# Gate scaling of half of each expert tile moved from ScalarE to GpSimd, between the tile's result scatters

## The reference

```python
x = x + 0.5 * ffn(layernorm(x))
x = x + attention(layernorm(x))
x = x + 0.5 * ffn(layernorm(x))
```

```python
topv_aK, topi_aK = jax.lax.top_k(x_aD @ router_DE, 2)
gates_Ea = sigmoid(masked scores).T          # -inf where not chosen
routed_in_EaD = x_aD[None] * gates_Ea[:, :, None]
h_EaF = silu(einsum('ead,edf->eaf', routed_in_EaD, w_in_eDF)) \
        * einsum('ead,edf->eaf', routed_in_EaD, w_swiglu_eDF)
out_aD = shared_out_aD + sum_over_e(einsum('eaf,efd->ead', h_EaF, w_out_eFD))
```

## Time and profile before

| what | value |
| --- | --- |
| runs | 1060.45 us median (1058.06 to 1062.33) |
| profiled execution | span 1057.9 us (the page gives no time beside it) |
| mean granted clock of TensorE | 0.915 |
| busy: PE, DVE, ACT, POOL | 864.0, 637.0, 562.7, 654.4 us |
| chain that ended last, by engine | PE 59%, ACT 11%, DVE 10%, unknown 10%, issue 5%, POOL 3% |

### The profile page before, as it was taken

The page is one execution under the profiler, slowest core; times in us unless marked ns, Lnnn a source line. Parts: engine busy times, 40 slices in busy tenths (PEclk is TensorE's granted clock), DMA queues, the critical chain, the costliest instruction groups (busy, mean ns, idle before and its releaser), DMA issues.

```text
span 1057.9 us, 19428 instructions
## 1 busy us (share of the span) xinstructions
PE 864.0 (82%) x5857; PEld 744.1 (70%) x5857; DVE 637.0 (60%) x2022; ACT 562.7 (53%) x1678; POOL 654.4 (62%) x669
## 2 busy tenths in 40 slices
PE   4655665658898888837999999997698988898898
PEld 3544555557888888833777776776598888898787
DVE  6644655454555555425798988885555554564586
ACT  4321422205655565528988888872165655565432
POOL 4656366453676776666088887666447666676551
PEclk9877787788999999978999999997889999899989
DMA  9511011043333333225012211111433233232484
GB/s 230 170 39 46 26 46 43 33 79 90 86 84 89 88 86 84 80 74 160 1 57 77 75 59 39 37 41 36 89 80 94 83 87 92 81 84 74 128 255 125
DMA packets 112920, 88.01 MB, mean 83 GB/s; under 512 B 13426, under 2 KB 102132, under 8 KB 112820
## 3 DMA queue, kind: packets, MB, share of 16 engines
q1 hardware_dynamic: 94816, 51.08, 19.1%
q0 software_dynamic: 17280, 35.69, 10.3%
q10 hardware_dynamic: 724, 0.01, 0.0%
HBM read 43.68 MB, written 43.04 MB: 82 GB/s over the span
## 4 chain that ended last, share of the span: by engine, by line
PE 59%; ACT 11%; DVE 10%; another core or an unknown queue 10%; issue 5%; POOL 3%; DMA 2%; SPq 0%; ACTq 0%; DVEq 0%
PE bank L927 12%; PE bank L1391 5%; PE bank L911 5%; PE bank L1367 4%; PE bank L909 4%; PE bank L910 4%; PE bank L917 4%; PE bank L1377 3%; ACT XG L865 2%; POOL results L837 2%; ACT SG L884 2%; PE bank L720 2%; PE bank L650 2%; PE bank L206 1%
## 5 line engine op out<-in xcount | busy, mean ns | idle before, releaser
L837 POOL DMA_INDIRECT results<-YO,XS x284 | 306.0, 1077 | 167.6 <-ACT YO L876 95.4
L818 DVE TENSOR_TENSOR HT<-bank,SG 128x512 f32<-128x512 f32 x142 | 98.3, 692 | 181.9 <-PE bank L911 88.3
L408 POOL DMA_INDIRECT pairs<-PAY,POS x128 | 126.5, 988 | 97.8 <-DVE POS L241 60.6
L909 PE MATMUL bank<-XSH,WX 128*128 128x256 f32 x568 | 175.2, 309 | 3.8 <-issue 3.7
L1017 POOL DMA_INDIRECT pairs<-PAY,POS x128 | 136.2, 1064 | 63.1 <-issue 32.9
L910 PE MATMUL bank<-XSL,WX 128*128 128x256 f32 x568 | 162.9, 287 | 3.8 <-issue 3.7
L911 PE MATMUL bank<-XSH,WX 128*128 128x256 f32 x568 | 162.7, 287 | 0.7 <-issue 0.4
L927 PE MATMUL bank<-WOE,HT 128*128 x1136 | 156.8, 282 | 0.2
L927 PEld LDWEIGHTS bank<-WOE,HT 128*128 128x128 f32 x1136 | 140.1, 194 | 5.0 <-issue 1.0
L865 ACT ACTIVATE XG<-XS 128x128 f32<-128x128 f32 x284 | 113.7, 402 | 21.6 <-DMA XS<-pairs 21.5
L910 PEld LDWEIGHTS bank<-XSL,WX 128*128 128x128 f32 x568 | 111.0, 195 | 5.4 <-issue 5.3
(11 more groups left out here) (197 smaller groups left out, 1825.3 us busy)
## 6 DMA issues: line engine op xcount, KB each, us to landing
XS<-pairs SPq DMA_DIRECT2D x142, 130.0 KB
Y<-results SPq DMA_DIRECT2D x32, 256.0 KB
YF<-results SPq DMA_DIRECT2D x32, 256.0 KB, 4.2
results<-YO,XS POOLq DMA_INDIRECT x284
pairs<-PAY,POS POOLq DMA_INDIRECT x256
out<-X SPq DMA_DIRECT2D x16, 256.0 KB, 3.0
pairs<-pad_rows SPq DMA_DIRECT2D x16, 130.0 KB
pairs<-pad_rows SPq DMA_DIRECT2D x1, 1040.0 KB
```

Source lines behind the costliest of these rows:

```text
L408: pool.indirect_dma_start(pairs, bass.IndirectOffsetOnAxis(ap=POS[:, b % RB, j, c:c + 1], axis=0), PAY[:, b % RB, c, j, :], None).then_inc ...
L818: dve.tensor_tensor(HT[:, i % 2, :], bank[4 + i % 2][:, :], SG[:, i % 2, :], ALU.mult)\
L837: pool.indirect_dma_start(results, bass.IndirectOffsetOnAxis(ap=XS[:, u, j, AT_DEST:AT_DEST + 1].bitcast(U32), axis=0), YO[:, u, j, :], No ...
L909: pe.matmul(ps, WX[:, i % 2, 1, w], hi, start=True, stop=False)
```

## The change

In both expert stages the gate scaling of each tile's second half (j = 1) is taken from ScalarE and given to GpSimd, as a `tensor_scalar` multiplication. ScalarE keeps the first half. On GpSimd the multiplication of tile i + 5 stands between the two scatters of tile i; those of the first five tiles stand ahead of all scatters. XG grows from two to three buffers. TensorE's transposes wait for both engines, by a semaphore for each, and GpSimd waits for the rows (xs_loaded) and for the transposes that last read its XG buffer (xs_turned).

```diff
--- before.py
+++ after.py
@@ -145,7 +145,7 @@
             "table_done pads_known pads_written padded "
             "std1 stats1 normed xt_turned xt_copied xt_split scored topped gate_raw gated picked ranked "
             "rank_taken pay1 pay2 placed up0 up1 silu0 silu1 hid0 hid1 down shared_added xt_high weights_high "
-            "xs_scaled xs_turned xs_high xs_low e_weights e_up0 e_up1 e_silu e_hid e_down e_out "
+            "xs_scaled xs_scaled2 xs_turned xs_high xs_low e_weights e_up0 e_up1 e_silu e_hid e_down e_out "
             "summed a_added a_stats a_log a_rstd a_shift a_normed a_turned a_copied q_made k_made v_made "
             "q_ready k_ready v_ready weighed updated r_stats r_log r_rstd kept_split combined").split())
         x_loaded = sems("x_loaded", len(GROUPS))
@@ -761,7 +761,7 @@
                 mem = ctx if ffn else own
                 XS = sb(f"XS{ffn}", [P, XB, 2, ROW], mem=mem)
                 YO = sb(f"YO{ffn}", [P, XB, 2, D], mem=mem)
-                XG = sb(f"XG{ffn}", [P, 2, 2, D], mem=mem)
+                XG = sb(f"XG{ffn}", [P, 3, 2, D], mem=mem)
                 XSH = sb(f"XSH{ffn}", [P, 2, 2 * P], F32R, mem=mem)
                 XSL = sb(f"XSL{ffn}", [P, 2, 2 * P], F32R, mem=mem)
                 WX = sb(f"WX{ffn}", [P, 2, 2, 2 * F], F32R, mem=mem)
@@ -830,13 +830,29 @@
 
                 @block.gpsimd
                 def _(pool):
-                    for i in range(NT):
+                    def scale(i):
+                        pool.wait_ge(xs_loaded[slot(i)], 16 * (turns(i) + 1))
+                        if i >= 3:
+                            pool.wait_ge(k["xs_turned"], done + i - 2)
+                        pool.tensor_scalar(XG[:, i % 3, 1, :], XS[:, slot(i), 1, 0:D],
+                                           XS[:, slot(i), 1, AT_GATE:AT_GATE + 1], None, ALU.mult)\
+                            .then_inc(k["xs_scaled2"], 1)
+
+                    def scatter(i, j):
                         u = slot(i)
-                        pool.wait_ge(k["e_out"], done + i + 1)
-                        for j in range(2):
-                            pool.indirect_dma_start(
-                                results, bass.IndirectOffsetOnAxis(ap=XS[:, u, j, AT_DEST:AT_DEST + 1].bitcast(U32), axis=0),
-                                YO[:, u, j, :], None).then_inc(y_sent[u], 16)
+                        if j == 0:
+                            pool.wait_ge(k["e_out"], done + i + 1)
+                        pool.indirect_dma_start(
+                            results, bass.IndirectOffsetOnAxis(ap=XS[:, u, j, AT_DEST:AT_DEST + 1].bitcast(U32), axis=0),
+                            YO[:, u, j, :], None).then_inc(y_sent[u], 16)
+
+                    for i in range(-5, NT):
+                        if i >= 0:
+                            scatter(i, 0)
+                        if i + 5 < NT:
+                            scale(i + 5)
+                        if i >= 0:
+                            scatter(i, 1)
 
                 @block.sync
                 def _(sp):
@@ -859,11 +875,10 @@
 
                 @block.scalar
                 def _(act):
-                    def scale(i, j):
-                        if j == 0:
-                            act.wait_ge(xs_loaded[slot(i)], 16 * (turns(i) + 1))
-                        act.activation(XG[:, i % 2, j, :], XS[:, slot(i), j, 0:D], ACT.Copy,
-                                       scale=XS[:, slot(i), j, AT_GATE:AT_GATE + 1]).then_inc(k["xs_scaled"], 1)
+                    def scale(i):
+                        act.wait_ge(xs_loaded[slot(i)], 16 * (turns(i) + 1))
+                        act.activation(XG[:, i % 3, 0, :], XS[:, slot(i), 0, 0:D], ACT.Copy,
+                                       scale=XS[:, slot(i), 0, AT_GATE:AT_GATE + 1]).then_inc(k["xs_scaled"], 1)
 
                     def high(i):
                         act.wait_ge(k["xs_turned"], done + i + 1)
@@ -876,20 +891,17 @@
                         act.activation(YO[:, slot(i), :, :].rearrange("p j d -> p (j d)"), bank[6 + i % 2][:, 0:2 * D],
                                        ACT.Copy, scale=0.5).then_inc(k["e_out"], 1)
 
-                    scale(0, 0)
-                    scale(0, 1)
+                    scale(0)
                     for i in range(-2, NT + 1):
                         if 0 <= i < NT:
                             act.wait_ge(k["e_up0"], done + i + 1)
                             act.activation(SG[:, i % 2, :], bank[2 + i % 2][:, :], ACT.Silu).then_inc(k["e_silu"], 1)
                         if i + 3 < NT:
-                            scale(i + 3, 0)
+                            scale(i + 3)
                         if i + 2 < NT:
                             high(i + 2)
                         elif ffn and i < NT:
                             act_kept_high(act, EARLY + i + 2 - NT, EARLY, KH)
-                        if i + 3 < NT:
-                            scale(i + 3, 1)
                         if 0 <= i - 1 < NT:
                             send(i - 1)
 
@@ -912,9 +924,10 @@
                             mm.then_inc(k[f"e_up{g}"], 1)
 
                     def turn(i):
-                        pe.wait_ge(k["xs_scaled"], 2 * (done + i) + 2)
+                        pe.wait_ge(k["xs_scaled"], done + i + 1)
+                        pe.wait_ge(k["xs_scaled2"], done + i + 1)
                         for j in range(2):
-                            mm = pe.transpose(chunk(bank[i % 2], j), XG[:, i % 2, j, :], ident[:, :])
+                            mm = pe.transpose(chunk(bank[i % 2], j), XG[:, i % 3, j, :], ident[:, :])
                         mm.then_inc(k["xs_turned"], 1)
 
                     def down(i):
```

## The result

The changed kernel takes 1114.86 us (median of 4 runs, 1109.05 to 1118.86) against 1060.6 us before (median of 4 runs, one more than in the section on the kernel before): a ratio of 1.048, 95% interval 1.043 to 1.053. The forecast was 1073 us with a range up to 1090. The direction was right, the size was not: 12 us forecast, 54 measured. Of the seven runs of the kernel before that stand beside the last four experiments one took 2032.86 us, and the ratios leave it out.

What follows compares the result with a forecast made beforehand. No engine was full, GpSimd nearest to it; the multiplication would make GpSimd pace-setter at 3.20 us per tile. The stages' 6.7 and 5.8 us raised the span from 1057.9 to 1070.4, plus 2.55 for the runs' median: 1073 us, range 1026 to 1090.

Steps and rivals of the forecast that it cites:

- the prediction's own chain: Expert stages: from one multiplication's end, transposes, XSH, XSL, CAST, held-up scatter to 2.84 us, next multiplication to 3.20 per tile.
- the collision: Expert stages: VectorE's CAST, 1.31 to 1.99 us after the multiplication, holds up GpSimd's first scatter, ending at 2.84; chance 0.46.
- the stalls of every fifth tile: Kernel before, expert stages: TensorE's signals arrive up to 4.6 us late, GpSimd waits 1.77 us for a YO copy.
- the nine last steps: End of each expert stage: last five tiles' scatters without multiplications between them, nine steps of 0.97 + 0.30, 11.4 us.
- the prediction's sum without a collision: GpSimd's own work in the expert stages: two scatters, multiplication and gaps, 2.77 us per tile.
- Rival A: Expert stages: the CAST misses the scatter, period 2.77 to 3.0 us, time 1033 us at 2.90, 1016 at 2.77; chance 0.28.
- Rival B: Expert stages: TensorE's late signals stay, period 3.29 us, +24 us, 1085 us; chance 0.13 with all that is slower still.
- The port rule of the Trainium skill: VectorE and GpSimd's shared ports lock exclusively per instruction; scatter runs wholly after the CAST, period 3.44, 1105 us; chance 0.02.
- My 222.6 us per stage: Each expert stage between first and last scatter: 66 x 3.20 = 211.2 plus 11.4 us, 6.7 and 5.8 more than before.

Runs made afterwards that it cites:

- the copy variant: The changed kernel, but GpSimd copies the second half of a tile's rows instead of multiplying it, those gates left out: 1006.12 us, ratio 1.081 to the kernel before.

## Why the prediction was wrong

**What failed** is the term "I take 0.35, with 0.21 and 0.47 as the ends" for the multiplication on GpSimd. It measured 0.61, outside of both bounds. They came from a copy and an addition, and by the runs of 64 and 128 columns a tensor_scalar on GpSimd costs 2.5 ns per column where the copy costs 0.8. By the prediction's own chain 0.61 gives 2.84 + 0.01 + 0.61 = 3.46 and a time of 1107 us. The upper end of the range, 1090, was the 0.47 carried through.

**The rest of the miss**, 0.06 us per tile and 8 us, is in three small terms: the transposes start 0.14 after the multiplication where I put 0.07, the operation after a scatter starts at 0.03 instead of 0.01, and the XSH copy follows the transposes by 0.45 instead of 0.48, which gives a little back. The scatter after an operation takes 1.02 instead of 0.97; the earlier trace rows had it at 1.04 behind the addition, and I overlooked it. It is hidden in the collision, since it moves the next scatter's start but not the CAST's end.

**What held.** GpSimd sets the pace; TensorE waits for it in each tile; the multiplication's end fixes the phase; the CAST starts at 1.35 (forecast 1.31) and is under way when the next first scatter starts; that scatter ends 0.84 to 0.85 after the CAST; the stalls of every fifth tile go; the clock stays at 1.00; the nine last steps have no multiplication. With the CAST taken away the period is 3.12, and the prediction's sum without a collision, with 0.61, 1.02 and the two gaps as measured in it, is 3.11.

**Rival A** failed in the changed kernel, but more narrowly than the prediction had it. It let the CAST miss from 0.12 after the scatter's start on, 0.25 us later than forecast. The runs put the limit at the scatter's start itself: a CAST that began with the scatter cost it nothing (the copy's 214.95), and so did CASTs from 0.09 to 0.14 after it in the kernel before. The CAST's start at 1.35 was only 0.15 before that (332.07 against 332.22); it held in each steady tile, and in the copy variant, with 0.10, two tiles near the start of the first stage fell out of it. **Rival B** failed, the stalls are gone. The port rule of the Trainium skill ("SBUF — State Buffer", section "SBUF: two separate sides"), read as in the prediction, with a scatter that does its whole 0.97 after the CAST, is against the rows of the changed kernel as well: 0.84.

**What I had read wrongly before it**: that the kernel before stalls by itself. It does so where it takes 1060 us, and not where it takes 928. I could not have known it from one trace, but I had a sign: waits of ScalarE and VectorE with "remote" as their end, on a single core. It changes what the forecast means: 12 us were so few only because the stalls had already slowed the kernel before. My 222.6 us per stage, set against 181.0 and 180.0, would have been 84 us, where 127 were measured. What makes TensorE's signals late there stays open, also whether it is the chip or another condition of those runs, and so does whether a break between scatters would help.

## What to carry to other kernels

An operation moved to an engine that "has time" costs its whole duration once that engine's round, gaps included, is as long as the pace-setter's; here GpSimd was busy 76% of the time and had nothing left. Its price must be read for the very instruction: a copy took 0.30 us and a multiplication by a column 0.61. Before work goes to GpSimd, look at which VectorE copies will stand beside its scatters, since each may hold one of them up (by 0.4 us per tile here, for a CAST of 0.68). And measure the kernel before beside the experiments: stalls that no row explains may be missing there.

## What the runs showed of the hardware

- GpSimd, 128 columns of float32: copy 0.30 us, product of two inputs with one broadcast 0.41, tensor_scalar by a constant 0.55, by a column 0.61; 64 columns by a column 0.45.
- Whether a CAST on VectorE (0.68 us) holds up an indirect scatter (0.97 us) goes by when it starts. Begun 0.15 before the scatter, the scatter takes 1.37 and ends 0.84 after the CAST. Begun with it (the copy's 214.95) or 0.14 after it (261.66), it costs the scatter nothing. Still running 0.85 after the scatter's start (CAST until 330.96, scatter from 329.85), it holds the scatter, which takes 1.23 and ends 0.12 after the CAST. Begun 0.57 after it, the CAST is held up instead, 0.90. The multiplication on GpSimd is open to the CAST too: 1.14 instead of 0.61.
- After a compute operation GpSimd's next scatter starts at 0.17 to 0.19 instead of 0.30. It takes 1.02 instead of 0.97 behind the multiplication, 0.98 behind the copy and 0.97 behind the memset.
- The same program took 1060 us in the runs beside the prediction and 928 to 930 on the two chips of the experiments. Of 132 us, 123 lie in stretches where waits for TensorE's signals that its rows don't explain are there in the one case and missing in the other.
